# Latent attention: the next batch's low keys at three steps of a batch instead of one, its query rows rounded in two halves

## The reference

```
kv_r = _apply_rope(kv_c, sin_k[None], cos_k[None])
q_r = jnp.einsum('bshq,hqr->bhsr', q_big, W_qr)
k_r = jnp.einsum('bld,hdr->bhlr', kv_r, W_kr)
scores = jnp.einsum('bhsr,bhlr->bhsl', q_r, k_r)
attn = jax.nn.softmax(scores, axis=-1)
ctx_c = jnp.einsum('bhsl,bld->bhsd', attn, kv_r)
```

## Time and profile before

| | us |
|---|---|
| median of 3 runs (lowest, highest) | 1552.97 (1552.28, 1555.54) |
| span of the profiled execution, first to last instruction | 1563.7 |
| PE busy | 1450.8 (93%) |
| DVE busy | 935.0 (60%) |
| POOL busy | 789.6 (50%) |
| ACT busy | 630.5 (40%) |
| the latent attention's loop over batches in this execution | about 468 to 970 |

### The profile page before, as it was taken

One profiled execution on the slowest core, in us unless ns is written; L12 is line 12 of the kernel. 1 busy time (PEld: TensorE's weight loads), 2 busy tenths in 40 slices (PEclk: granted clock), 3 DMA queues, 4 the chain that ended last, 5 costly groups with the idle time before them and its releaser, 6 DMA issues. The chain is left out here.

```text
span 1563.7 us, 21601 instructions
## 1 busy us (share of the span) xinstructions
PE 1450.8 (93%) x7635; PEld 1100.7 (70%) x7635; DVE 935.0 (60%) x1619; ACT 630.5 (40%) x1151; POOL 789.6 (50%) x621
## 2 busy tenths in 40 slices
PE   7788999899989999999999998988999998899998
PEld 4455566566646676676766755567988887899998
DVE  2752112466686768767686753577878774444554
ACT  2432221344423434424244342456666653333333
POOL 3732002367647769768677673057565551233332
PEclk9998999799999899989989999999999999999999
DMA  8014113510011101011010000101010001443441
GB/s 306 1 44 142 34 38 86 179 53 24 1 39 57 58 0 58 1 58 58 1 57 7 14 1 14 71 28 33 23 55 1 28 1 42 120 119 120 121 121 52
DMA packets 60321, 88.66 MB, mean 57 GB/s; under 512 B 7556, under 2 KB 44612, under 8 KB 60230
## 3 DMA queue, kind: packets, MB, share of 16 engines
q1 hardware_dynamic: 59206, 85.82, 17.2%
q0 software_dynamic: 1024, 1.64, 0.4%
HBM read 81.92 MB, written 5.41 MB: 56 GB/s over the span
## 5 line engine op out<-in xcount | busy, mean ns | idle before, releaser
L1007 ACT ACTIVATE prob<-PS 121x800 f32<-121x800 f32 x192 | 158.1, 837 | 254.0 <-PE PS L2041 238.3
L1405 DVE TENSOR_REDUCE mx<-PS 128x1 f32<-128x482 f32 (+1 forms) x312 | 186.7, 649 | 56.6 <-PE PS L2019 54.6
L622 POOL TENSOR_TENSOR e_wl<-e_wf,e_wh 128x768 fp32r<-128x768 f32 x33 | 71.0, 2151 | 174.4 <-ACT e_wh L905 152.6
L717 POOL TENSOR_TENSOR hT<-hT,prob 121x800 f32<-121x800 f32 x56 | 109.7, 1958 | 71.1 <-ACT prob L1007 68.9
L2018 PE MATMUL PS<-kth,qs 128*128 128x482 f32 (+1 forms) x312 | 131.5, 422 | 13.7 <-DVE mx L1405 10.3
L2056 PE MATMUL PS<-prob,kvn 121*64 121x400 f32 (+1 forms) x768 | 136.1, 503 | 0.9 <-ACT prob L1007 0.9
L717 POOL TENSOR_TENSOR xc<-xc,prob 121x800 f32<-121x800 f32 x56 | 114.8, 2050 | 30.3 <-ACT prob L1007 25.8
L2019 PE MATMUL PS<-kl,qm 66*128 66x482 f32 (+1 forms) x312 | 125.4, 402 | 0.0
L2038 PE MATMUL PS<-qs,kth 128*121 128x400 f32 (+1 forms) x384 | 113.1, 377 | 3.1 <-ACT prob L1007 2.4
L2041 PE MATMUL PS<-qm,kl 66*121 66x400 f32 (+1 forms) x384 | 105.4, 357 | 0.0
L2056 PEld LDWEIGHTS PS<-prob,kvn 121*64 121x64 f32 (+1 forms) x768 | 52.3, 137 | 71.2 <-issue 69.0
(11 more groups left out here) (301 smaller groups left out, 3650.1 us busy)
## 6 DMA issues: line engine op xcount, KB each, us to landing
e_wb<-routing SPq DMA_DIRECT2D x32, 400.0 KB, 3.9
wgu<-in_L_ffn_gate_up_proj SPq DMA_DIRECT2D x8, 1024.0 KB, 14.3
krt<-in_ctx_T SPq DMA_DIRECT2D x8, 722.0 KB, 4.1
ksw<-in_ctx_Tswap SPq DMA_DIRECT2D x8, 722.0 KB, 5.8
wdn<-in_L_ffn_down_proj SPq DMA_DIRECT2D x8, 512.0 KB, 7.9
wq<-in_L_ffn_Wq SPq DMA_DIRECT2D x4, 1024.0 KB, 5.3
wo<-in_L_ffn_Wo SPq DMA_DIRECT2D x4, 1024.0 KB, 5.7
e_wf<-in_L_ffn_Wg SPq DMA_DIRECT2D x32, 128.0 KB, 2.2
```

The source lines that it names most:

```text
L622: pool.tensor_tensor(m["wl"][:, slot], m["wf"][:, slot], m["wh"][:, slot].bitcast(fp32), ALU.subtract).then_inc(ms["wlo"], 1)
L717: pool.tensor_tensor(acc, acc, prob[:, n % RING], ALU.add).then_inc(xb["ap"], 1)
L1007: act.activation(prob[0:k, n % RING], PS[0:k, 2 * (n % 2):2 * (n % 2) + 2, 0:GC], ACT.Exp).then_inc(xb["ex"], 1)
L1405: dve.tensor_reduce(mx3[:, m, g:g + 1], PS[:, 4 + k % 3, 0:SEG[g][1]], AX.X, ALU.max).then_inc(xb["free"], 1)
```

## The change

The work is the same; it is put at other steps, and one instruction becomes two.

- ACT: `high_queries` takes a half i of the query rows, 800 columns. At step 2 stay group 0 of the high keys and half 0; half 1 comes after step 3's exponential; group 1 after step 4's; group 2 after step 6's.
- DVE: group 0 of the low keys stays at step 2; group 1 comes at step 4, ahead of that step's maxima (units 2 and 3), and group 2 at step 7, ahead of the maxima of units 8 to 10.
- PE: unit 0 waits for half 0 alone, unit 6 (step 6) for half 1.

The steps at which keys are split are written out once per engine:

```diff
-            def high_queries(b):
-
-                if b >= 2:
+            def high_queries(b, i):
+
+                if b >= 2 and i == 0:
                     act.wait_ge(xb["s"], SP_ * (b - 1))
-                act.activation(qm2[:, b % 2], qs[0:DC + 2, b].rearrange("p h s -> p (h s)"), ACT.Copy,
-                               scale=keep[:, 0:1]).then_inc(xb["q2"], 1)
+                act.activation(qm2[:, b % 2, i * HQ // 2:(i + 1) * HQ // 2],
+                               qs[0:DC + 2, b, i * H1 // 2:(i + 1) * H1 // 2].rearrange("p h s -> p (h s)"),
+                               ACT.Copy, scale=keep[:, 0:1]).then_inc(xb["q2"], 1)
@@
                     if s == 2 and more:
                         high_keys(b + 1, 0)
-                        high_queries(b + 1)
+                        high_queries(b + 1, 0)
+                    if s == 3 and more:
+                        high_queries(b + 1, 1)
+                    if s == 4 and more:
                         high_keys(b + 1, 1)
+                    if s == 6 and more:
                         high_keys(b + 1, 2)
@@
-                    if s == 2 and more:
-                        for g in range(3):
-                            low_keys(b + 1, g)
+                    if s in (2, 4, 7) and more:
+                        low_keys(b + 1, (2, 4, 7).index(s))
@@
                 if u == 0:
                     pe.wait_ge(xb["one"], min(b + 1, 2))
-                    pe.wait_ge(xb["q2"], 1 if b == 0 else b + 2)
-                if b == 0 and u == MA - 1:
-                    pe.wait_ge(xb["q2"], 2)
+                    pe.wait_ge(xb["q2"], 2 * b + 1)
+                if u == MA - 1:
+                    pe.wait_ge(xb["q2"], 2 * b + 2)
```

More of the change, by code:

```diff
@@ L1026, in _ @@
                     high_keys(0, 2)
-                act.activation(qm2[:, 0, i * HQ // 2:(i + 1) * HQ // 2], qs[0:DC + 2, 0, i * H1 // 2:(i + 1) * H1 // 2].rearrange("p h s -> p (h s)"),
-                               ACT.Copy, scale=keep[:, 0:1]).then_inc(xb["q2"], 1)
+                high_queries(0, i)
             for b in range(B + 1):
```

## The result

| | before | after | ratio, 95% interval |
|---|---|---|---|
| timed, median (range), us | 1552.62 (1549.47 to 1555.54) | 1585.94 (1576.94 to 1596.29) | 1.0233 [1.0184, 1.0283] |
| timed again on another chip | 1550.79 | 1576.48 (1570.59 to 1583.62) | 1.0182 [1.0151, 1.0213] |
| profiled execution, span | 1563.7 | 1578.6 (its own time 1580.37) | |
| batches 1 to 6 in it | 386.10 | 407.18 | |

The ratios are those on record, a little above the quotients of the medians beside them (1.0215 and 1.0166). The change makes the kernel 1.8 to 2.3% slower, some 25 to 33 us. The forecast was +11 us, 1564, with a range to 1573. The sign was right, the size too small by half or more, and 1585.94 lies outside the range.

The account below looks back on a forecast made before the run. PE's stops and the slow clock behind them were taken to bound the kernel. Batches 1 to 6 at 60.1 + 2.15 + 3.9 = 66.2 us add 11, batch 0 nothing: 1564 us, range 1538 to 1573.

Parts of the forecast that it names:

- What bounds the loop: How long PE stops in batches 0 to 6, and whether the clock falls behind each stop, decides the change.
- Group 1's new wait: Low keys on DVE at step 4 wait for ACT's high keys; PE stops 2.15 us at unit 5, batches 0 to 6.
- T: Start of step 4's exponential on ACT; group 1 of the low keys was to start 1.36 us after it.
- D: Length of group 1 of the low keys on DVE, taken as 2.0 us because it meets POOL's addition.
- The clock: Behind PE's stops the clock halves to 1.2 GHz; each slow stretch costs 3.9 us, one in each of batches 1 to 6.
- rival A: PE's stops come mostly without a slow stretch: 1538 us with none, 1550 with half of them; chance 0.17.
- SP and POOL: Later loads make POOL wait about 10 us at step 7; costed at nothing, bound 3 us a batch.
- Rival C: Load waits aren't absorbed, reaching ACT's ring or DVE's addition of step 15: 3 us a batch, 1580 us; chance 0.05.
- The stops of 1.71 and 1.77 us go: PE's stops at unit 17 (step 10) in batches 2 and 4 vanish, DVE's step 8 running beside an idle POOL.
- Batch 0: Gains 0.9 us at unit 0, pays up to 2.15 at unit 5; in sum 0, within 2 us.
- The baseline: Profiled execution before is 10.7 us above the median 1552.97; same difference assumed after, so 1574.7 becomes 1564.
- Halves and group 2 at step 7: Two 800-column query copies on ACT cost nothing at step 3; DVE's group 2 at step 7 was also taken as nothing.

Follow-up runs that it names:

- experiment 4: Changed kernel with value rows loaded ahead of krt and ksw and group 1 of high and low keys back at step 2: 0.9894; changed kernel rerun unaltered: 1.0182.
- experiment 5: Kernel before with only SP's order changed, value rows loaded ahead of krt and ksw: 0.9952 of before.
- Experiment 10: Changed kernel with value rows loaded first, and POOL's addition of step 4 waiting for step 5's exponential: 0.9971 of before.
- experiment 1: Changed kernel with SP loading the value rows ahead of krt and ksw: 1.0118 of before.
- experiment 9: Changed kernel with value rows loaded first, plus ten matmuls of zeros ahead of unit 5 in batches 1 to 6: 0.9995 of before.
- experiment 3: Changed kernel with group 1 of high and low keys back at step 2, loads left late: 1.0062 of before.
- experiment 8: Kernel before with only SP's loads of krt, ksw and value rows held until step 7's exponential: 1.0044 of before.
- experiment 7: Kernel before with only the query rows rounded in two halves, the second at step 3: 0.9999 of before.

## Why the prediction was right and wrong

**What bounds the loop: right.** PE's stops and the clock behind them are the loss: with both causes out, it is gone. The stop-free batch, which I had worked out as 60.1 us, is 60.6 in experiments 4 and 5.

**Group 1's new wait: right in place, length and cause.** It starts at T + 1.37 (forecast T + 1.36), D is 2.10 to 2.38 (forecast 2.0), the stop 2.07 to 2.35 (forecast 2.15) in batches 1 to 6. In batch 0 the stop is not of that size: D is 1.95, but the stop 0.40. The second profile of the changed kernel has it in four batches of six, so "in every batch" was too strong. Experiment 10 shows that D comes from POOL's addition. The Trainium skill (SBUF — State Buffer, "Who interferes with whom") gives DVE and GpSimd a shared read port that one of them holds exclusively; by its rule the prediction had D at 2.1, and this case's 2.11 us against 0.65 agrees.

**The clock: right that it falls, mis-sized.** It fell behind each of the six stops in the first profile of after, behind three of the four of 2.0 to 2.1 us in the second, and behind five of six in that of experiment 1; rival A, mostly without slow stretches, is out. It was no more than likely beforehand: the loop in the Trainium skill's section (TensorE: Matmul & The Clock Gate, "HAM oscillation — how this bites in real kernels") waits about 3 to 5 us in each tile, so that "by that all six pay" doesn't follow for a stop of 2.15. The price of a slow stretch goes with its length. In experiment 1, read in slices of 0.5 us, a batch without one takes 62.4 us, those with 4 us of slow clock 63.3 and 63.5, with 7 us 64.9 and 64.7, with 10.5 us 66.3. The forecast's 3.9 us was taken from stretches of 10.5 and is right for those: batch 6 of after, which has the stop at unit 5 and no late loads, has 11 us of slow clock and takes 66.30, where the sum had 66.2. The mean of the five in experiment 1 is 2.1 us. By the timed runs of experiments 1 and 9 it is 1.2% of 1545 us over six batches, 3.1 us each; the profiled execution of experiment 1 was the fastest of its six.

**SP and POOL: the step that failed.** "I cost this at nothing, with a bound of 3 us a batch": POOL's lateness was seen (10 us forecast, 10 to 11.5 measured), and that it has caught up by step 16 is right (it idles 5.67 us at 580.84). But what stands on DVE between step 8 and step 16, and shares the port with a POOL that no longer has gaps, wasn't listed: the addition of tile 11 at step 12, with all of step 13's maxima behind it. I looked for who waits for POOL's results, and nobody did; what is held is an instruction that needs nothing of POOL. Rival C named ACT's ring and the addition of step 15, at 3 us a batch and 1580 us, and had a chance of 0.05: the time is nearly that, the instruction is another. By the profiles, batches 1 to 6 are 17 to 22 us longer than in experiment 1 (402.13 and 407.18 against 384.97), 2.9 to 3.7 us a batch; by the timed runs it is 10 to 18 us. With the loads early the kernel stands at 1.0118, which is 1571 us: this term alone took the time out of the range. With group 1 out of the way, by experiments 4 and 3: group 1 back at step 2 with the loads late is 1.0062, with the loads early 0.9894, so 1.7% for the late loads; put on the kernel before, 0.44% (experiment 8), or 0.9% against experiment 5, where its own stops are gone. Group 1 costs 2.2% with the loads early. Both together are 2.9 to 3.4% above 0.9894, somewhat less than the sum of 3.9. "The stops of 1.71 and 1.77 us go" was right for the first profile, with worse ones in their place; the second has one of 1.80 at step 10 of batch 4.

**Batch 0: mis-sized.** Forecast 0 within 2 us, measured +5.6 in the profiled pair. The 0.9 us at unit 0 came (the stop is 1.73 instead of 2.44, 0.7), but batch 0 has the longest stop of step 13, 3.00 us, with a slow stretch behind.

**The baseline: mis-sized.** I took the profiled execution of before as 10.7 us above the median and the difference as the same for both. It wasn't: after's span is 7.3 us below its median. The record shows that this execution of before was an unusual one: its mean granted clock was 0.964, and that of 69 of 70 other runs of before on three chips is 0.965 to 0.984 (the seventieth took 7180 us and is left out), where after's 0.963 lies amid the 0.955 to 0.970 of its own ten runs. In the 23 runs of before on one chip the time goes from 1535.68 us at a clock of 0.984 to 1558.15 at 0.965. So the forecast took off the cost of stops and slow clock of which most runs of before have less. How much of the 7 us between 1571, the kernel with the loads early, and the forecast's 1564 that explains was not measured. In the profiled pair the loop from batch 0 is 26.7 us longer, of which batches 1 to 6 have 21.1 against the 11 forecast; what lies outside the loop is 11.8 shorter, of which no cause was looked for.

**Halves and group 2 at step 7: right.** Halves 0.9999. Group 2's place costs nothing that shows: with groups 0 and 1 at step 2 and the loads early, nothing above 0.6 us is left. What it cost, it cost through the loads behind its semaphore. "What goes is the queue of two groups ahead of unit 0" named only half of what the stops of 2.1 us need (experiment 5).

## What to carry to other kernels

A moved instruction moves its semaphore too: follow each queue that waits on it to the transfers behind it, then to the engine that waits for these, and ask what that engine now does without a gap, and what on another engine shares a port with it. The victim need not depend on anything that became late. In a loop in which PE is nearly always busy, count a stop of 2 us about twice, and nearly three times where a slow stretch of 10 us follows (66.30 - 60.6 for 2.13, batch 6 of after). One profile of each kernel is one draw: compare its mean clock with that of the timed runs before you subtract from it. Look first at whether the load can be issued ahead of the wait: two lines of SP's order were worth 0.5% on the kernel before, and with two of the three edits kept, 1.1%.

## What was not expected of the hardware

**DVE can lose the port to POOL twice in a row.** In batch 1 of after DVE's addition stands from 561.54, while POOL's L664 runs until 562.22; it doesn't end 0.98 later, near 563.2, but at 564.92, 0.5 us behind the first of the two additions that POOL started at 562.17 (each 2.25). In experiment 8 it is the same, 4.27 us for an instruction of 0.98. Against a POOL without gaps such an instruction costs up to two of POOL's, not one. The Trainium skill (same page and section) says that whoever issues first holds the port; by that DVE, in the queue since 561.54, would have gone ahead of the addition at 562.17. These rows show otherwise, though the profile's spans of POOL are rough, and nothing run here tells why.

**Short stops bring the half clock, and not each time.** In the kernel after the clock fell at each of the stops of 2.07 to 3.00 us, for 3.5 to 11 us, and at those of 1.07, 1.73 and 1.88 us too, not at 0.99; 1.71 had left it alone, and so did the one of 2.28 us in experiment 1. In experiment 7 it fell behind 1.53 and not behind 1.67 and 1.77. The length of the stop alone doesn't say. Ten small matmuls of zeros in the stop, 1.87 us of work, kept it at 2.4 GHz and gave back 1.2% of the whole time (experiment 9).

**Open.** Why the order of SP's loads frees DVE's addition of step 0 (experiment 5) was not followed further back, nor why the stops of 1.7 us at step 10 vanish with it. Nor was why both causes removed is 0.6% faster than experiment 5 with the same 60.6 us a batch: the profiles put 3.8 us of it ahead of batch 1's values, and that of experiment 5 is itself 5 us below its median.
